# A mixture-of-experts kernel on one core: weighted sum as quarter-width matmuls over 32-partition result transfers, freed tile fetches, and an early table load on ScalarE

## The reference, cut to what matters

```
x = x + _L0_xattn_ref(_layernorm(x), L0_xattn_k, fside_S2_0, ctx_2048, ctx_2048, 8)   # long convolution, as matmuls
x = x + _L0_ffn_ref(_layernorm(x), ...)                                               # base plus 2 of 16 low-rank experts
x = x + _L1_xattn_ref(_layernorm(x), ctx_2048, ...)                                   # attention of 16 heads
x = x + _L1_ffn_ref(_layernorm(x), ...)                                               # 32 experts, 4 for each row

def _L1_ffn_ref(hidden, router_w, expert_bias, gate_w, up_w, down_w, shared_...):
    scores = jnp.sqrt(jax.nn.softplus(flat @ router_w.T))
    _, idx = jax.lax.top_k(scores + expert_bias, 4)
    topv = jnp.take_along_axis(scores, idx, axis=1)
    topv = topv / (topv.sum(axis=-1, keepdims=True) + 1e-20)
    out  = sum over the row's 4 experts of topv * (silu(clip(x @ wg.T)) * clip(x @ wu.T)) @ wd.T
    return out + shared expert
```

## Time and profile before

| | us |
|---|---|
| median of the 3 runs (689.58, 691.42, 693.4) | 691.42 |
| the profiled execution | 689.39 |
| its span in the profile | 687.6 |

### The profile page before, as it was taken

How to read it: one execution, slowest core, us unless ns; L and a number is a source line. 1 busy time by engine, 2 the same in 40 slices (tenths; PEclk the granted TensorE clock), 3 DMA queues, 4 the chain that set the end, 5 groups by cost and what they waited for, 6 DMA issues and landing times.

```text
span 687.6 us, 14458 instructions
## 1 busy us (share of the span) xinstructions
PE 592.0 (86%) x4117; PEld 476.3 (69%) x4117; DVE 442.0 (64%) x1374; ACT 391.8 (57%) x1156; POOL 373.1 (54%) x527
## 2 busy tenths in 40 slices
PE   0588899999998899998899778785887999999985
PEld 0488777787776688777686556553666887788863
DVE  1546656777666876757756586276655777655576
ACT  1002366766777655784657886662534666677660
POOL 6837847457455565586735434614154555555560
PEclk9999999999999999999999999896789999999999
DMA  7989999999999996123323965876443555555599
GB/s 261 263 210 335 335 334 334 332 330 324 318 311 324 317 304 209 52 59 113 118 71 110 347 208 156 275 266 211 147 125 108 163 157 162 149 164 161 158 349 345
DMA packets 130204, 155.02 MB, mean 225 GB/s; under 512 B 15216, under 2 KB 117744, under 8 KB 129744
## 3 DMA queue, kind: packets, MB, share of 16 engines
q1 hardware_dynamic: 112000, 122.50, 59.0%
q0 software_dynamic: 7632, 20.98, 8.5%
q10 hardware_dynamic: 10496, 10.62, 4.9%
HBM read 53.92 MB, written 100.28 MB: 224 GB/s over the span
## 4 chain that ended last, share of the span: by engine, by line
PE 62%; DVE 13%; POOL 7%; ACT 7%; issue 6%; DMA 3%; another core or an unknown queue 1%; SPq 1%; ACTq 0%; DVEq 0%; POOLq 0%
PE ps L416 11%; PE pc L679 11%; PE pS L383 6%; PE pS L659 4%; POOL arena L1441 4%; PE ps L461 3%; PE ps L645 2%; PE po L630 2%; PE ps L488 2%; PE ps L522 2%; PE po L406 2%; PE ps L514 2%; PE ps L505 2%; PE ps L591 2%; DMA arena<-y_rows 2%
## 5 line engine op out<-in xcount | busy, mean ns | idle before, releaser
L679 PE MATMUL pc<-arena,tk 128*128 128x128 f32 x768 | 109.5, 296 | 13.3 <-POOL arena L1441 7.2
L679 PEld LDWEIGHTS pc<-arena,tk 128*128 128x128 f32 x768 | 97.7, 203 | 25.5 <-issue 13.3
L416 PE MATMUL ps<-arena,work 128*128 x380 | 102.2, 393 | 1.4 <-ACT work L1193 1.4
L1441 POOL TENSOR_TENSOR arena<-arena 128x512 f32<-128x512 f32 x64 | 90.2, 1423 | 21.8 <-ACT arena L1239 21.6
L1455 POOL DMA_INDIRECT expert_rows<-stage,ixl x64 | 63.6, 994 | 37.0 <-DVE ixl L1056 19.4
L1306 ACT ACTIVATE work<-pS,work 128x128 f32<-128x128 f32 x256 | 72.5, 369 | 4.4 <-DVE work L958 4.0
L416 PEld LDWEIGHTS ps<-arena,work 128*128 128x128 f32 x380 | 67.5, 198 | 7.5 <-issue 1.8
L755 DVE TENSOR_SCALAR work<-ps 128x256 f32<-128x256 f32 x95 | 40.1, 422 | 46.5 <-PE ps L416 44.7
L383 PE MATMUL pS<-arena,tk 128*128 x190 | 61.1, 404 | 8.1 <-ACT tk L1188 6.5
L1183 ACT ACTIVATE tk<-work 128x128 f32<-128x128 f32 x95 | 29.4, 310 | 57.7 <-DVE work L755 48.6
L958 DVE TENSOR_REDUCE work<-pS 128x4 f32<-128x512 f32 x64 | 43.9, 685 | 24.6 <-PE pS L659 21.3
(11 more groups left out here) (317 smaller groups left out, 1463.8 us busy)
## 6 DMA issues: line engine op xcount, KB each, us to landing
expert_rows<-stage SPq DMA_DIRECT2D x32, 2080.0 KB, 20.7
work<-expert_rows SPq DMA_DIRECT2D x95, 130.0 KB
arena<-in_w SPq DMA_DIRECT2D x16, 768.0 KB
stage<-xn_rows SPq DMA_DIRECT2D x64, 130.0 KB
xn_rows<-xnD ACTq DMA_DIRECT2D x16, 512.0 KB, 4.9
arena<-y_rows SPq DMA_DIRECT2D x8, 512.0 KB, 9.9
tk<-in_tk SPq DMA_DIRECT2D x1, 2048.0 KB, 10.0
work<-y_rows SPq DMA_DIRECT2D x4, 512.0 KB
```

What stands on the lines that cost most here:

```text
L416: i = pe.matmul(p[U * k:U * k + U, 0:256], xgT[n % 3][:, 128 * c + U * k:128 * c + U * k + U], arena[:, 256 * c:][:, bass.ds(e, 256)], sta ...
L679: i = pe.matmul(pv, tk[:, h, 128 * d:128 * d + 128], kvv[:, ci, :, :].rearrange("p b (i h j) -> p (b i) h j", i=8, h=8)[:, :, hl, :], star ...
L1441: pool.tensor_tensor(kv[kk % 4][:, c, half, :].rearrange("p (i h j) -> p i h j", h=8, i=8), i0, i1, ALU.mult).then_inc(s_kv, 1)
```

## The change

**Tile fetch.** The fetch brings 257 columns instead of 260, and DVE copies the places from column 256 to column 257 (a new instruction for each tile, behind line 757 of before). The scatter reads column 257, so the fetch of tile n waits only for DVE's copy of tile n - 12 (`s_ix`), no more for its scatter; DVE's copy waits for that scatter instead.

**Result transfers.** Each rank now goes into a quarter of the partitions: rank k into partitions 32k to 32k + 31, as four pieces of 512 KB, all 16 with the same line. Row p of a batch (p = 32j + i) of rank k lands in partition 32k + i. The 128 x 4096 blocks `ranks[g]`, one for each four batches, lie in `work` and in the first 12288 columns of `arena`, the weights of experts 0 to 15. The one wait for PE (`gone[16]` = 79 tiles) stands ahead of the first rank; the wait for all 95 is gone.

**Weighted sum.** For each batch DVE builds a matrix `mixes[b]` of 128 x 128 (16 new instructions in ticks 62 to 77, from `fold`, an identity folded four times, and `pT`, the weights brought into the partitions of their rank). PE then does 4 matmuls for each batch, one for each quarter j of the rows: stationary 128 x 32, moving 128 x 256, output in the 32 partitions of quarter j. One such matmul sums the four ranks. These are 64 matmuls; the 24 of before, the 24 diagonals of ACT and the 40 instructions of DVE go. DVE adds two batches at a time, 8 instructions of 128 x 512.

**ScalarE.** A tanh of one column ahead of ACT's first wait for data brings the table load with it. Two more edits concern the same places: the weights `qp` move from `arena` to `work`, and SP's wait for `s_swb` ahead of the expert weights goes.

```diff
+        accs = [*gbanks, *xbanks, po, banks.tiles[2], *ybanks]
...
+        mixes = [*(m[:, 4 * n:4 * n + 4, :].rearrange("p b e -> p (b e)") for m in (lg4, Sall, Ball) for n in range(4)),
+                 *(stage[:, n, 0:128] for n in range(4))]
+        gone = [EARLY + (NB * 128 * KT - EARLY * U + e * (U - 1)) // U for e in range(NE)]
+        ranks = [m.rearrange("p (j b d) -> p j b d", j=4, b=4)
+                 for m in (work[:, WORK - 4096:WORK], *(arena[:, 4096 * g:4096 * g + 4096] for g in range(3)))]
...
 tensor_program
+            pe.wait_ge(s_y, NT)
             pe.wait_ge(s_acc, NB)
+            for b in range(NB):
+                p = accs[b // 2]
+                if b % 4 == 0:
+                    pe.wait_ge(d_in[2 + b // 4], 48 + 16 * KT)
+                pe.wait_ge(s_dg, b + 1)
+                for j in range(4):
+                    i = pe.matmul(p[32 * j:32 * j + 32, 256 * (b % 2):256 * (b % 2) + 256], mixes[b][:, 32 * j:32 * j + 32],
+                                  ranks[b // 4][:, j, b % 4, :], start=True, stop=True)
+                if b % 2:
                     i.then_inc(s_yp, 1)
...
 vector_program
+                    if n >= NX:
+                        dve.wait_ge(d_y[(n - NX) % 4], 16 * ((n - NX) // 4 + 1))
+                    dve.wait_ge(d_g[n % 4], 16 * (n // 4 + 1))
+                    dve.tensor_copy(xg[n % NX][:, 257:258].bitcast(I32), xg[n % NX][:, 256:257].bitcast(I32)).then_inc(s_ix, 1)
...
+                for k in at(t, 57, 1, KT):
+                    for j in range(4):
+                        dve.tensor_copy(pT[32 * k:32 * k + 32, :, j], pk4[32 * j:32 * j + 32, :, k]).then_inc(*own.up())
+                    dve.wait_ge(*own.now())
+                for b in at(t, 62, 1, NB):
+                    if b >= 12:
+                        dve.wait_ge(d_sc[b - 12], 16 * SC[b - 12])
+                    dve.tensor_tensor(mixes[b].rearrange("p (j c) -> p j c", j=4), fold.unsqueeze(1).broadcast_to((128, 4, 32)),
+                                      pT[:, b, :].unsqueeze(2).broadcast_to((128, 4, 32)), ALU.mult).then_inc(s_dg, 1)
...
+            for n in range(NB // 2):
+                dve.wait_ge(s_yp, NT + n + 1)
+                dve.tensor_tensor(xs[:, 2 * n:2 * n + 2, :], accs[n][:, :].rearrange("p (b d) -> p b d", b=2),
+                                  xs[:, 2 * n:2 * n + 2, :], ALU.add).then_inc(s_acc, 1)
...
 scalar_program
+            act.wait_ge(s_pconst, 1)
+            act.activation(dall[:, 0:1], epsc[:, :], ACT.Tanh)
             act.wait_ge(d_id, 16)
...
 sync_program
                     if n >= NX:
-                        sp.wait_ge(d_y[(n - NX) % 4], 16 * ((n - NX) // 4 + 1))
+                        sp.wait_ge(s_ix, n - NX + 1)
-                    sp.dma_start(xg[n % NX], Xs[bass.ds(r, U), 0:260]).then_inc(d_g[n % 4], 16)
+                    sp.dma_start(xg[n % NX][:, 0:257], Xs[bass.ds(r, U), 0:257]).then_inc(d_g[n % 4], 16)
...
+                    sp.wait_ge(s_yp, gone[16])
                 sp.wait_ge(s_st, last[k])
-                if k == 1:
-                    sp.wait_ge(s_yp, NT)
-                    continue
+                yk = Yr[DUMP + NB * 128 * k:DUMP + NB * 128 * (k + 1), :].rearrange("(j p b) d -> p j (b d)", j=4, b=NB)
                 for g in range(4):
+                    sp.dma_start(ranks[g][32 * k:32 * k + 32, :, :, :].rearrange("p j b d -> p j (b d)"),
+                                 yk[:, :, 1024 * g:1024 * g + 1024]).then_inc(d_in[2 + g], 16)
```

More of the change, by code:

```diff
@@ L63 @@
 DUMP = 512
-SUMMED = {}
-for k in (3, 2):
-    for b in ENDV:
-        SUMMED[k, b] = NB + len(SUMMED) + 1
-for g in range(4):
-    for k in (1, 0):
-        for b in (b for b in ENDV if b // 4 == g):
-            SUMMED[k, b] = NB + len(SUMMED) + 1
-    for b in (b for b in ENDP if b // 4 == g):
-        SUMMED[0, b] = NB + len(SUMMED) + 1
 NX = 12
@@ L188, in build @@
         PT = [carve([128, 512]) for _ in range(3)]
+        qp = work[:, 4864:6912]
         o_ = [carve([128, 256])]
@@ L211, in build @@
         NY = len(y)
-        far = [arena[:, 6400 + 4096 * k:10496 + 4096 * k].rearrange("p (b d) -> p b d", d=256) for k in range(2)]
         st = {n: sb(f"st{n}", [128, 2, 16]) for n in "ABCD"}
@@ L1173, in tile_steps @@
             def tile_steps(t):
-                for c in at(t, 57, 2, 2 * NPS):
-                    k, b = 3 - c // NPS, ENDP[c % NPS]
-                    if c == 0:
-                        act.wait_ge(s_routed, 1)
-                    act.activation(diag[c], ident, ACT.Copy, scale=pk4[:, b, k:k + 1]).then_inc(s_dg, 1)
                 for n in at(t, 2, 1, NT):
@@ L1355, in scalar_program @@
                     tile_steps(i)
-            for c in range(2 * NPS, KT * NPS):
-                b, k = ENDP[(c - 2 * NPS) // 2], 1 - c % 2
-                act.activation(diag[c], ident, ACT.Copy, scale=pk4[:, b, k:k + 1]).then_inc(s_dg, 1)
             act.wait_ge(s_st, NT - 4)
@@ L1498, in sync_program @@
                         sp.wait_ge(s_uT, 2 * NP)
-                        sp.wait_ge(s_swb, 1)
                     sp.dma_start(wv_[:, 2 * i:2 * i + 2, :], a_w[2 * i:2 * i + 2].rearrange("e p n -> p e n")).then_inc(d_w, 16)
```

81 lines of the change are left out of this document (15 added, 66 removed).

## The result

| | before | changed |
|---|---|---|
| median, us | 690.57 (4 runs, 689.58 to 693.4) | 697.62 (4 runs, 696.61 to 701.48) |
| profiled execution, us | 689.39 | 696.69 |
| its span, us | 687.6 | 694.9 |

The changed kernel is slower: ratio 1.013, 95% interval 1.0075 to 1.0185, some 7.1 us. I had forecast 693.9, 2.5 us more than before: the time lies inside the range of 683.5 to 699.5, 3.7 us above the likeliest value. On the profiled executions, which the sum was made for, 2.5 us were forecast and 7.3 measured: 4.8 us have to be explained.

What follows compares the result with a forecast made beforehand. The end was taken as bound by 4.19 MB of results that couldn't be asked for earlier. Last landing 685.5 plus 5.9 for sums, less 1.3 for the table load, gave 690.1, 2.5 over 687.6: median 693.9, range 683.5 to 699.5.

Steps and rivals of the forecast that it cites:

- When the transfers start: End of loop: SP, freed by DVE's copy of tile 82, issues the first result transfer at 642.8, 8.9 us earlier.
- The 16 `mixes`, about 0.3 us each, and the copies into `pT` fall into ticks 56 to 77, where the 0.69 us cover them: Expert loop: DVE's idle 0.69 us before each tile hides this work, so it costs nothing.
- Then 8.39 MB take 40.6 us: Result transfers at 206 GB/s: data until 683.4, last rank landed at 685.5, against 681.7 before.
- the middle of the two bounds: Result transfers into 32 partitions: 206 GB/s, geometric middle between 413 (engine-bound) and 103 (partition-bound).
- The last sums: After rank 0 of group 3 lands: four blocks, DVE's last addition, issue and output transfer, together 5.9 us.
- the lower end: Last sums: a block of 4 quarter-width matmuls takes 0.51 us if quarters overlap fully, at most 0.86; 0.6 taken.
- Four blocks: 2.4 us: Last sums on PE: the last four batches, 0.6 us a block, start when rank 0 of group 3 is there.
- addition and output: Behind PE's last block: DVE's addition 0.68 us, SP's issue 0.1, output transfer 2.7; 3.5 us.
- The table load: Start: ACT's table load moves off the chain, from 6.65 to about 1 us; all 1.28 us arrive at the end.
- Full rate: Rival, result transfers: 32 partitions written as fast as others, PE bounds the end, 6.0 us less, 685.4; chance 0.30.
- Slowed scatters: Rival, last tiles: scatters take 11.3 us under load, deciding from 10.4; 5.4 us more, 696.8; chance 0.18.
- What I had named as signs: End: transfers at 200 to 290 GB/s for 35 to 40 us; PE idle before each block of 16 matmuls.

Runs made afterwards that it cites:

- the run with spread copies: Changed kernel, bounded tile-number loads, the 16 copies into `pT` one per tick (57 to 72), mixes from tick 74: 681.8 us, ratio 1.0086 to the kernel before.
- the run without copies on DVE: Changed kernel with rank k in partitions k, k + 4, ... and fitting weights sent through HBM instead of 16 DVE copies: 672.6 us, ratio 0.9963.
- the run with the short matmuls: The control plus 18 unread 128x256 matmuls on PE between its last tile and the sums: 684.58 us, ratio 1.0147 to the kernel before.
- The run with all ports: The control with rank k written to partitions k, k + 4, ... k + 124, weights not brought along: 674.4 us, ratio 0.9964 to the kernel before.
- the kernel before with the early load: Kernel before plus ScalarE's early tanh and bounded tile-number loads, nothing else of the change: 674.64 us, ratio 0.998.
- the control: Changed kernel with the four tile numbers loaded with bounds: 685.23 us, ratio 1.0122 to the kernel before; again on another chip 687.15 us, 1.0164.
- the third version: Strided ranks, weights through HBM, ranks 3 and 2 first, PE's wait at batch 12, tile-number loads ahead of fetch 68; against kernel before: 666.43 us, 0.9868.

## Why the prediction was right or wrong

**In short.** The mechanism was right: the result transfers run at half rate, and that makes the kernel slower. Three steps failed in size: the copies that were to be covered in the expert loop and weren't, the length of the transfers, and the clock of PE at the last sums, which the sum left out.

**When the transfers start: wrong by 2.35 us.** 641.5 was forecast (642.8 less the table load), 643.85 measured. That SP is freed by DVE's copy of tile 82 held: 2.06 us from the clip of that tile to the first transfer, 1.8 forecast. The step that failed is "The 16 `mixes`, about 0.3 us each, and the copies into `pT` fall into ticks 56 to 77, where the 0.69 us cover them". Four copies of 32 partitions take 0.78 to 0.99 us in one tick, more than the 0.69 us of idle time, and the next clip stands behind them. I had counted the copies as one kind of work with the mixes and not set the four of a tick against the idle time of one. What they cost is 0.75 us by the run with spread copies, and 0.9 by the run without copies on DVE (8.21 against 9.12), on the faster chips.

In the pair of the forecast the same five tiles lost 1.6 us (10.49 against 8.91). The other 0.7 to 0.8 stays open: DVE stood idle in front of three of the five clips, and no run here shows what held them. The lag of 0.3 us ahead of tile 55 is DVE's copy of the places or chance (on another chip this copy took some 1 us there), and the 0.5 behind tile 60 stands where the first mixes are; no run takes these apart.

**The rate: right in kind, up to 2.0 us too short.** Results at 206 GB/s and scatters at 80 on top of them were forecast, 286 in all; the trace shows 256 to 259 in all. By the run with the short matmuls group 3 was there at most 44.7 us behind the first transfer, where 42.7 were forecast, so the results alone came at 197 GB/s or more (8.39 MB in 44.7 less 2.1 us). The step that failed is "Then 8.39 MB take 40.6 us": up to 42.6. That the middle of the two bounds fell on the half was luck, since the forecast gave no reason for it out of its own rows: a full rate and a quarter have a half between them. The run with all ports shows the cause by itself. The Trainium skill's page "SBUF — State Buffer", section on Door 1, has the rule that bears on it, that 32 neighbouring partitions reach half of the ports. The traces agree: 257 GB/s in all for neighbours and 412 for spread partitions, with scatters in both. The Trainium skill has about 218 GB/s for such a transfer, and the results alone came at 197 or more. The run with all ports adds that 32 partitions spread over all of SBUF, which aren't among the ranges that the Trainium skill measures in that section, reach the full rate.

**The last sums: right in kind, wrong in size.** PE waits for the transfers, and its blocks follow. A block of four quarters takes 0.43 us at full clock, less than the 0.51 that I had as the lower end. That end was built from passes of 128 columns. The kernel before has the right row: full-width matmuls of 256 columns, which follow one another every 0.43 us.

```profile
671.86 0.59 PE L695 MATMUL ps<-arena,Ball 128*128 128x256 f32 x2
672.29 1.03 PE L695 MATMUL ps<-arena 128*128 128x256 f32 x4
```

So four quarters take what one full matmul takes: they overlap fully. By the Trainium skill's page "TensorE: Matmul & The Clock Gate", section on packing small matmuls, a block would have been 0.52 us when worked out from my 0.51; from 0.43 the same rule gives an estimate of 0.44, and the trace agrees with that.

The step that failed is "Four blocks: 2.4 us". It took PE to be waiting for the last group and said nothing of the clock. In the changed kernel PE had been idle for 11.2 of the 12.4 us ahead of the sums (4.61 and 6.60 in its timeline) and started at half clock, so it was behind the transfers from group 0 on and waited for none of the later groups. With the clock kept, it would have ended 1.1 us earlier (46.6 instead of 47.7 us behind the first transfer).

**The sum again.** Start 2.35 us later; last landing up to 2.0 later; the four blocks at full clock 1.9 instead of 2.4 us, so -0.5; the clock 1.1; addition and output 3.4 instead of 3.5, so -0.1. That makes 4.85 us, where 4.8 had to be explained. The landing and the blocks are known only together, as 1.5 us, since PE didn't wait for group 3 in the run with the short matmuls. So half of the error is the late start, of which 0.75 to 0.9 us are shown to be the copies, and the other half lies behind the first transfer.

**The table load: right as far as it can be seen.** 1.28 us were forecast, and 1.64 and 1.61 are seen at the first convolution and at tile 0. Some 0.4 of that isn't the load's: POOL's last step of the first scale begins at 6.31 us before and at 5.90 in the changed kernel.

**The rivals.** Full rate fell: 32 neighbouring partitions moved 257 GB/s in all, not 413. With spread partitions the kernel gains 2.4 us over the one before (ratio 0.9964), less than the 6.0 that I had worked out for this rival. The part behind the clip of tile 82 came as worked out there: 42.0 us to the end of the span (628.68 to 670.7), where 9.6 us of blocks and 3.5 behind them had given 41.9. What is missing is in the loop, which took 146.6 us from tile 0 to tile 82, against 144.8 in the kernel before with the early load on another chip; for the other half of the missing 3.6 us these runs name no cause. Slowed scatters: they did slow down. The scatter of tile 89, which ACT's last copy waits for, took 8.3 us (666.74 to 675.06) instead of 6.7, and that of tile 87 took 9.5 (663.41 to 672.95). All of this is below the 10.4 from which this rival decides, and PE waited for the transfers.

```profile
663.41 0.96 POOL L1353 DMA_INDIRECT y_rows<-xnA,work  x1 [4.66 <-ACT xnB L1174]
...
666.74 0.96 POOL L1353 DMA_INDIRECT y_rows<-xnC,work  x1 [1.09 <-ACT tk L1174]
```

```profile
672.95 0.38 ACT L1174 ACTIVATE xnA<-pS 128x256 f32<-128x256 f32 x1 [4.87 <-DMA y_rows<-xnA,work]
...
675.06 0.38 ACT L1174 ACTIVATE xnC<-pS 128x256 f32<-128x256 f32 x1 [0.76 <-DMA y_rows<-xnC,work]
```

What I had named as signs was half right: the stretch at 200 to 290 GB/s is there, PE's idle time in front of each group is not, because the slow clock hid it. It shows in the run where the clock was kept, for groups 1 and 2.

## What to carry to other kernels

A transfer into a block of 32 neighbouring partitions gave away over a third of the rate here, with 512 KB in each (257 instead of 412 GB/s); if a layout needs one rank in a quarter of the partitions, take every fourth partition and permute the small operand instead. Set what is added to a tick of a tight loop against the idle time of that one tick, in the order in which its engine does it, not against the mean of many. Take the price of a matmul from rows with the same number of columns, not from shorter ones. Before you price the work of an engine that waits, look at its granted clock, and then at whether the time saved only becomes a wait for the next transfer: here 3 us of slower matmuls were worth 1.

## What the runs showed of the hardware

Quarters that alternate in one queue gain little: 266 to 273 GB/s between 640 and 670 us, against 253 to 269 in the control with one quarter after another. PE's granted clock stayed at 1.00 over idle times of 0.68 and 1.33 us between groups of sums and was at 0.50 after one of 6.76 us. In the third version the last tiles of the loop had idle times of 0.62 and 1.09 us, and there the clock was at half for PE's last tile (1.21 us for what takes 0.69) and part of group 0; so a single idle time doesn't tell the clock. Other queues pay for a slow destination too: the scatter of tile 89, which writes to HBM, took 8.5 us in the control and 6.1 with all ports, with the transfer engines just as full (1.03 and 1.04). Whether they wait in the transfer engines behind the longer packets or for something else wasn't tried.
